# A two-layer block with gated attention and mixtures of experts: how the rows of the sparse layer travel to their experts and back

## The chip, the cores and the metric

One core of one Trainium2 chip. The metric is the device time of one execution in microseconds, the median of the runs shown. Engines by the names of the profile: PE (TensorE, matmuls), PEld (its weight load), DVE (VectorE), ACT (ScalarE), POOL (GpSimd), SP (SyncE, which issues most DMAs). A row "SPq" or "PEldq" is the sequencer of that engine.

## The reference

`x` is 4 x 256 rows of 256 numbers (T = 1024 rows). Four steps follow, each of the form x = x + tanh(g) * f(layernorm(x)): an adjacency attention and a mixture of 8 experts with a shared one (layer 0), then a latent attention of 16 heads and a mixture of 16 experts with a shared one (layer 1). The last step is the one that the change concerns:

```python
scores = jax.nn.sigmoid(x @ gate_w)
_, selected = jax.lax.top_k(scores + expert_bias[None, :], 2)
top_scores = jnp.take_along_axis(scores, selected, axis=1)
top_scores = top_scores / (top_scores.sum(-1, keepdims=True) + 1e-20)
shared = jax.nn.silu(x @ shared_gate_w) * (x @ shared_up_w) @ shared_down_w
comb = jnp.zeros((T, E), jnp.float32).at[jnp.arange(T)[:, None], selected].add(top_scores)
for e in range(E):                     # E = 16, F = 128
    g, u = jnp.split(x @ experts_gate_up[e], 2, axis=-1)
    routed = routed + comb[:, e:e + 1] * (jax.nn.silu(g) * u @ experts_down[e])
return shared + routed
```

## The kernel before

Everything is written out by hand: one program per engine, with semaphores between them, so the order of each engine is the order of the code. `x` lives in SBUF as 8 tiles of 128 rows (`NT` = 8); a half is 4 tiles. Layer 0 and the attention of layer 1 run first. The attention is a loop over 8 pairs of heads in 12 slots each (`run_pairs`); functions in a dictionary are hung into single slots of the first or last pass. Slot 11 of the last pass holds the last output projection (`project`, L1374), its result is added to x by DVE (L1770).

The sparse layer of the second half of the program has these parts.

- **Norm and routing, by halves.** `Norm.stats`, `act_root`, `scale` (rows `xn`), `pe_transpose` (L323), `act_high` and `low` (`xT_h`, `xT_l`, two parts of fp32r that together keep the precision). `Router.pe_logits` (L374), a copy by ACT (L380), `pe_turn_logits` (L387), a sigmoid by ACT, and `choose1` on DVE, which leaves two one-hot rows for each token (`ohs`) and their sum `chosen`. In the last pass, `attention_to_ffn` hangs in slot 11: it issues the first half's logits and the gate and up matmuls of the shared expert (`ffn1.gateup`, L696) in front of the last projection.
- **Ranks and places.** `rank_pe` counts with triangular matmuls, once for both halves, how many earlier rows chose the same expert. `place` on DVE turns this into a slot in a list in which each expert owns whole blocks of 128 slots (`NBLK` = 31 blocks in all, the most that can be needed), and writes `in_blk` and `spread`, from which `rows_pe1` (L491) sums a table `rows_u`: for each block the 128 rows of x. `owners` gives for each block its expert's offset in the weights (`owner_i`).
- **Shared expert.** `gateup`, `act_silu`, `hidden`, `low`, `pe_down` (L721), `add` (L673) for each half. PE starts the blocks when the second `add` is done (`ffn1.acc`).
- **Blocks.** SP has stored the normed rows twice in DRAM (`xn_rows`). For each block POOL gathers 128 rows by index from it (L826, four buffers `moe_x`), PE transposes them (`turn`, L859), multiplies by gate and up (`gateup`, L870), transposes the hidden rows (`turn_hidden`, L879) and projects down (`down`, L886); ACT and DVE stand between. The weights of all experts are in SBUF, and PE finds a block's by a register. Four registers at a time are loaded from SBUF (L897) in front of `gateup` of blocks 0, 4, 8, ...; each value is checked at run time against its limits. PE issues block b's `gateup`, `turn_hidden(b-1)`, `down(b-2)`, `turn(b+2)`. ACT writes the result (`moe_y`, four buffers, L927) and SP stores it to DRAM (`y_rows`, L842).
- **End.** When all stores have landed, POOL gathers 16 times 128 rows by slot, two for each token tile (L835). DVE multiplies them by the routing weights and adds them to x (`combine`, L964, L969), and SP stores the output in four pieces (L979).

## Time and profile before

| | us |
|---|---|
| median of 3 runs | 642.78 |
| the runs | 644.35, 642.78, 639.86 |
| the profiled execution, its own time | 644.12 |
| its span, first to last instruction | 642.3 |

| engine | busy us | share of the span |
|---|---|---|
| PE | 539.5 | 84% |
| PEld | 392.2 | 61% |
| DVE | 433.3 | 67% |
| ACT | 293.1 | 46% |
| POOL | 158.2 | 25% |

The busy times are those of the whole span, in which stages with different limits follow one another. The page gives further the chain of work that ended last, with the share of each engine in it, and the DMAs with their time from issue to landing. The trace behind it can be asked for stretches and single lines.

### The profile page before, as it was taken

What the parts mean: (1) busy time and instruction counts of PE and PEld (TensorE: products, weight loads), DVE (VectorE), ACT (ScalarE), POOL (GpSimd) and SP (SyncE); (2) the same over time, 40 slices, a digit from 0 to 9 for tenths busy, and PEclk for the clock granted to TensorE, in tenths of its full rate; (3) what the DMA queues carried; (4) which work ended last, traced back from release to release, by engine and by line L of the source; (5) the groups of instructions that cost most, each with busy time, mean ns of one, the idle gap of its engine ahead of it and who ended that gap; (6) DMA issues with size and microseconds to landing.
All of it is one profiled execution on the core that took longest, in us unless ns stands there. A gap on an engine that the chain in (4) does not pass through costs nothing.

```text
span 642.3 us, 9412 instructions
## 1 busy us (share of the span) xinstructions
PE 539.5 (84%) x2822; PEld 392.2 (61%) x2822; DVE 433.3 (67%) x1152; ACT 293.1 (46%) x753; POOL 158.2 (25%) x161
## 2 busy tenths in 40 slices
PE   6797999987889989999999999999988672799900
PEld 3574687764678865666666666666656442677700
DVE  5997289985465656979787979797878557322213
ACT  3844433335365523545554655464547340255400
POOL 1043156642245512101010101010000011455254
PEclk9868899997889999999999999999998856699965
DMA  7669022221313220101010101000045110134233
GB/s 261 206 225 337 21 73 74 75 66 36 113 35 98 82 82 25 34 26 35 24 33 24 33 24 33 24 0 1 1 180 229 65 66 3 47 112 127 75 106 115
DMA packets 25440, 51.80 MB, mean 81 GB/s; under 512 B 4211, under 2 KB 15421, under 8 KB 25024
## 3 DMA queue, kind: packets, MB, share of 16 engines
q1 hardware_dynamic: 23152, 47.20, 22.2%
q0 software_dynamic: 2256, 4.20, 2.5%
q8 instruction: 16, 0.26, 0.2%
q14 instruction: 16, 0.13, 0.1%
HBM read 40.63 MB, written 12.71 MB: 83 GB/s over the span
## 4 chain that ended last, share of the span: by engine, by line
PE 63%; DVE 19%; ACT 7%; issue 6%; DMA 2%; POOL 2%; POOLq 0%; DVEq 0%; SPq 0%; ACTq 0%
PE bank L1306 10%; PE bank L1324 9%; PE bank L696 8%; PE bank L870 5%; PE bank L1347 5%; PE bank L1357 3%; PE bank L721 3%; DVE left L1704 3%; PE bank L1374 2%; PE bank L886 2%; DVE best L1699 2%; PE bank L1205 2%; PE bank L1338 2%; PE bank L1214 2%; PE bank L374 1%
## 5 line engine op out<-in xcount | busy, mean ns | idle before, releaser
L1522 ACT ACTIVATE silu<-bank,negm 128x256 f32<-128x256 f32 x128 | 59.4, 473 | 37.5 <-DVE negm L1751 37.3
L1530 ACT ACTIVATE probsT<-bank 128x512 f32<-128x512 f32 x64 | 38.4, 600 | 60.9 <-PE bank L1347 60.9
L1324 PE MATMUL bank<-qr,att_w_raw 128*64 128x512 f32 (+1 forms) x192 | 61.9, 605 | 1.2 <-issue 1.2
L1168 POOL TENSOR_TENSOR att_w_l<-att_w_raw,att_w_h 128x384 fp32r<-128x384 f32 x16 | 16.2, 1020 | 167.0 <-ACT att_w_h L1546 167.0
L618 POOL TENSOR_TENSOR ffn_w_l<-ffn_raw,ffn_w_h 128x512 fp32r<-128x512 f32 x30 | 38.7, 1290 | 72.0 <-ACT ffn_w_h L630 57.1
L642 ACT ACTIVATE hid_h<-hid 128x512 fp32r<-128x512 f32 x30 | 18.9, 631 | 67.8 <-DVE hid L657 48.4
L1759 DVE TENSOR_SCALAR hid<-silu,rden 128x256 f32<-128x256 f32 x128 | 47.6, 414 | 2.3
L1347 PEld LDWEIGHTS bank<-ident,hid 128*128 128x128 f32 x256 | 29.2, 142 | 28.3 <-issue 19.2
L1347 PE MATMUL bank<-ident,hid 128*128 128x128 f32 x256 | 40.8, 283 | 5.6 <-DVE hid L1759 2.8
L1751 DVE TENSOR_REDUCE negm<-bank 128x2 f32<-128x512 f32 x64 | 43.6, 682 | 2.2 <-PE bank L1339 1.3
L624 POOL TENSOR_TENSOR ffn_w_l<-ffn_raw,ffn_w_h 128x256 fp32r<-128x256 f32 x30 | 22.9, 765 | 88.4 <-ACT ffn_w_h L634 88.4
L696 PE MATMUL bank<-xT_h,ffn_w_h 128*128 128x512 f32 x120 | 44.2, 454 | 0.0
L826 POOL DMA_INDIRECT moe_x<-xn_rows,route_rows x31 | 31.1, 1004 | 43.3 <-DVE route_rows L545 16.9
L696 PE MATMUL bank<-xT_l,ffn_w_h 128*128 128x512 f32 x120 | 41.8, 432 | 0.0
L1770 DVE SCALAR_TENSOR_TENSOR x<-bank,tg,x 128x512 f32<-128x512 f32 x32 | 23.8, 744 | 21.5 <-PE bank L1374 21.5
L1338 PE MATMUL bank<-ks_h,qs 128*128 128x256 f32 x128 | 36.9, 310 | 1.6 <-ACT silu L1522 1.6
L721 PE MATMUL bank<-ffn_w_h,hid_h 128*128 128x256 f32 x120 | 31.5, 294 | 7.9 <-DVE x L673 4.4
L870 PE MATMUL bank<-moe_w,moe_xT 128*128 x124 | 34.5, 403 | 3.9 <-issue 2.4
L1737 DVE TENSOR_TENSOR qr<-bank,cosq 128x512 f32<-128x512 f32 x48 | 33.0, 687 | 5.0 <-PE bank L1306 4.6
L655 DVE TENSOR_TENSOR silu<-silu,bank 128x512 f32<-128x512 f32 x22 | 15.1, 686 | 31.3 <-ACT rows L447 16.5
L951 DVE COPY moe_hidT<-bank 128x128 f32<-128x128 f32 x31 | 9.0, 292 | 39.3 <-PE bank L879 39.3
L1357 PE MATMUL bank<-probsT,kv 128*64 128x256 f32 x256 | 35.4, 398 | 0.0
(217 smaller groups left out, 1357.9 us busy)
## 6 DMA issues: line engine op xcount, KB each, us to landing
ffn_raw<-in_w_ffn SPq DMA_DIRECT2D x30, 256.0 KB, 2.6
pair_w<-in_pair_w SPq DMA_DIRECT2D x8, 768.0 KB, 5.6
moe_w<-in_w_moe SPq DMA_DIRECT2D x2, 3072.0 KB, 14.0
folds<-att_w_raw SPq DMA_DIRECT2D x6, 896.0 KB, 6.8
att_w_raw<-folds SPq DMA_DIRECT2D x12, 384.0 KB, 3.1
y_rows<-moe_y SPq DMA_DIRECT2D x31, 128.0 KB, 1.8
ffn_raw<-in_w_ffn SPq DMA_DIRECT2D x30, 128.0 KB, 2.3
xn_rows<-xn SPq DMA_DIRECT2D x4, 512.0 KB, 3.5
```

Of the source, the lines that this page charges most:

```text
L618: nc.gpsimd.tensor_tensor(wt_l[b][:, 0:GU], raw[b][:, 0:GU], wt_h[b][:, 0:GU], ALU.subtract).then_inc(self.wgl, 1)
L696: last = nc.tensor.matmul(bank[2 * st.b + g][:], wp[st.b][:, (2 * kt + g) * P:(2 * kt + g + 1) * P], xp[:, kt, st.hf * 512:(st.hf + 1) * 512],
L721: last = nc.tensor.matmul(bank[4 + t // 2][:, (t % 2) * D:(t % 2 + 1) * D], hp[st.b][:, t * P:(t + 1) * P], wp[st.b][:, GU:WC], start=(sel ...
L870: last = nc.tensor.matmul(bank[2 + b % 2][:, 0:2 * P], xgT[b % 2][:, k, :], cells[:, bass.ds(cell + k * 2 * P, 2 * P)], start=(k == 0), st ...
L1306: last = nc.tensor.matmul(bank[bk][:], m_of(wp[b], k, j), xp[:, k, c * 512:(c + 1) * 512], start=(m == 0), stop=(m == 5))
L1324: last = nc.tensor.matmul(bank[2][cols, :], g_of(w_raw[b], 2 * j + w)[:, cols], qr[n % JT][:, w, :], start=(first and w == 0), stop=(not f ...
L1338: nc.tensor.matmul(o, q, ks_h[:, keys], start=True, stop=False)
L1347: last = nc.tensor.matmul(bank[6][:, (2 * h + k) * P:(2 * h + k + 1) * P], pn[u % 2][:, h, k * P:(k + 1) * P], ident[:], start=True, stop= ...
L1357: last = nc.tensor.matmul(bank[7][h * C:(h + 1) * C, 0:S], kv[:, 2 * b + k, 0:C], pT2[b % 2][:, h, k, :], start=(k == 0), stop=(k == 1), s ...
L1522: last = nc.scalar.activation(ex[u % 2][:, h, :], bank[4 + u % 2][:, h * S:(h + 1) * S], ACT.Exp, bias=negm[:, u % 2, h:h + 1], accum_out= ...
L1751: nc.vector.tensor_reduce(negm[:, u % 2, :], bank[4 + u % 2][:].rearrange("p (h n) -> p h n", h=2), AX_X, ALU.max, negate=True).then_inc(s ...
L1759: last = nc.vector.tensor_scalar(pn[u % 2][:, h, :], ex[u % 2][:, h, :], rden[:, u % 2, h:h + 1], None, ALU.mult)
```

## The change

The attention is untouched. In the sparse layer:

- The normed rows are no longer stored twice in order and gathered by block. DRAM now holds `xn_slots`, 16 regions of 1024 rows, one for each expert. Each row is scattered by POOL to its expert's region at its rank (16 indexed DMAs from SBUF, two for each tile). The place needs only ranks, so it is worked out by halves (`slots`), and `rank_pe` runs by halves too.
- A block is then 128 consecutive rows of a region. SP loads it with a plain DMA whose address is in a register (`row_at`, from a longer `owners`), four registers at a time.
- As a region is not full, it is cleared before: 8 DMAs of 2 MB from one blank tile, issued by SP, two in front of the loop over pairs and six in it.
- A block's result is scattered by POOL with the table `rows_u` straight to the token's row of `y_rows`; lanes without a row have an index over the limit and are left out. The 16 gathers at the end become 8 plain DMAs of 256 KB from SP.
- `rows_u` is still summed by PE, now in bf16 from two values in one matmul (`blk_val`), and is needed by the first scatter of results only. `spread` is one operation instead of 16.
- The register loads have no run-time check, and PE's next four stand behind `down(b-2)`.
- The last projection of the attention comes in front of the first half's logits and shared-expert matmuls, the orders of PE, ACT and DVE around it are as in the diff, and the expert weights come in one DMA instead of two. PE waits for `ffn1.acc` as before.

```diff
-        xn2 = nc.dram_tensor("xn_rows", (2 * T, D), F32, kind="Internal").ap()
-        y2 = nc.dram_tensor("y_rows", (NBLK * P, D), F32, kind="Internal").ap()
+        xn2 = nc.dram_tensor("xn_slots", (E1 * T, D), F32, kind="Internal").ap()
+        y2 = nc.dram_tensor("y_rows", (2 * T, D), F32, kind="Internal").ap()
...
-        def rank_pe(pe):
...
+        def rank_pe(pe, hf):
+
+            pe.wait_ge(s_chosen, hf + 1)
+            ps, t0 = ranks[hf], 4 * hf
+            nc.tensor.matmul(ps[:, 0:4, :], tri[:, 0:P], chosen[:, t0:t0 + 4, :], start=True, stop=False,
+                             skip_group_check=True)
...
+        def slots(dve, seq, hf):
+
+            ts = slice(4 * hf, 4 * hf + 4)
+            dve.wait_ge(s_rank, hf + 1)
             dve.wait_ge(s_cst, 16)
-            ranks = bank[0][:, 0:NT * E1].rearrange("p (t e) -> p t e", e=E1)
-            count = bank[0][:, NT * E1:(NT + 1) * E1]
+            seq.link(nc.vector.tensor_tensor(
+                capv[:, ts, :], ranks[hf][:, 0:4, :],
+                cst[:, C_CAP:C_CAP + E1].unsqueeze(1).broadcast_to([P, 4, E1]), ALU.add))
+            seq.link(nc.vector.tensor_tensor(
+                smul[:, ts, :, :], ohs[:, ts, :, :], capv[:, ts, :].unsqueeze(2).broadcast_to([P, 4, 2, E1]),
+                ALU.mult))
+            cs = slice(8 * hf, 8 * hf + 8)
+            seq.link(nc.vector.tensor_reduce(slot_of[:, cs], smul[:, ts, :, :].rearrange("p t j e -> p (t j) e"),
+                                             AX_X, ALU.add))
+            nc.vector.tensor_copy(slot_u[:, cs], slot_of[:, cs]).then_inc(s_slot, 1)
...
-            for c in range(2 * NT):
-                last = nc.vector.tensor_scalar(spread[:, c, :], cst[:, C_LANE:C_LANE + P], lane[:, c:c + 1],
-                                               cst[:, C_ROW + c:C_ROW + c + 1], ALU.is_equal, ALU.mult)
-            last.then_inc(s_spread, 1)
...
+            nc.vector.tensor_tensor(
+                spread[:], cst[:, C_LANE:C_LANE + P].unsqueeze(1).broadcast_to([P, 2 * NT, P]),
+                lane[:].unsqueeze(2).broadcast_to([P, 2 * NT, P]), ALU.is_equal).then_inc(s_spread, 1)
...
-            def clear(self, pool):
-                for i in range(NGB):
-                    nc.gpsimd.memset(xg[i][:], 0.0).then_inc(s_xg0, 1)
-
-            def gather(self, pool, b):
-                if b >= NGB:
-                    pool.wait_ge(s_mt, b - NGB + 1)
+            def place(self, pool, hf):
+
+                pool.wait_ge(s_clr, 16 * CLEARS)
...
+                for t in range(4 * hf, 4 * hf + 4):
+                    for c in (2 * t, 2 * t + 1):
+                        nc.gpsimd.indirect_dma_start(
+                            xn2, bass.IndirectOffsetOnAxis(ap=slot_u[:, c:c + 1], axis=0), xn[:, t, :], None,
+                            bounds_check=E1 * T - 1, oob_is_err=False).then_inc(s_xsc, 16)
+
+            def scatter(self, pool, b):
...
                 nc.gpsimd.indirect_dma_start(
-                    xg[b % NGB][:], None, xn2, bass.IndirectOffsetOnAxis(ap=rows_u[:, b:b + 1], axis=0),
-                    bounds_check=2 * T - 1, oob_is_err=False).then_inc(s_xg[b % NGB], 16)
-
-            def fetch(self, pool):
-                for i in range(NYB):
-                    pool.wait_ge(s_ysc[i], 16 * len(range(i, NBLK, NYB)))
-                for t in range(NT):
-                    for j in range(2):
-                        nc.gpsimd.indirect_dma_start(
-                            yback[j][:, t, :], None, y2,
-                            bass.IndirectOffsetOnAxis(ap=slot_u[:, 2 * t + j:2 * t + j + 1], axis=0),
-                            bounds_check=NBLK * P - 1, oob_is_err=False).then_inc(s_back[t // 2], 16)
-
-            def store(self, sp, b):
-                sp.wait_ge(s_my, b + 1)
-                sp.dma_start(y2[b * P:(b + 1) * P, :], ysb[b % NYB][:]).then_inc(s_ysc[b % NYB], 16)
+                    y2, bass.IndirectOffsetOnAxis(ap=rows_u[:, b:b + 1], axis=0), ysb[b % NYB][:], None,
+                    bounds_check=2 * T - 1, oob_is_err=False).then_inc(s_ysc[b % NYB], 16)
 
             def prog_pool(self, pool):
+                self.place(pool, 0)
+                self.place(pool, 1)
                 pool.wait_ge(s_row_of, 1)
...
-                self.fetch(pool)
+                for b in range(NBLK):
+                    self.scatter(pool, b)
+
+            def values(self, eng, at, b, top):
+                n = min(4, NBLK - b)
+                _, got = nc.values_load_multi_w_load_instructions(
+                    at[0:1, b:b + n], engines=[eng], min_val=0, max_val=top,
+                    skip_runtime_bounds_check_because="the value is held under its limit by the minimum before it")
+                return {b + i: v for i, v in enumerate(got)}
+
+            def prog_sp(self, sp):
+                sp.wait_ge(s_owner, 1)
+                row = {}
+                for b in range(NBLK):
+                    if b % 4 == 0:
+                        row.update(self.values(mybir.EngineType.SP, row_at, b, E1 * T - P))
+                    if b == 0:
+                        sp.wait_ge(s_xsc, 16 * 2 * NT)
+                    if b >= NGB:
+                        sp.wait_ge(s_mt, b - NGB + 1)
+                    sp.dma_start(xg[b % NGB][:], xn2[bass.ds(row[b], P), :]).then_inc(s_xg[b % NGB], 16)
...
+                pe.wait_ge(s_cell, 16)
                 pe.wait_ge(s_owner, 1)
-                cell = {}
+                cell = self.values(mybir.EngineType.PE, cell_at, 0, (E1 - 1) * CELL)
                 self.turn(pe, 0)
...
-                    if b % 4 == 0 and b < NBLK:
-                        n = min(4, NBLK - b)
-                        _, got = nc.values_load_multi_w_load_instructions(
-                            owner_i[0:1, b:b + n], engines=[mybir.EngineType.PE], min_val=0,
-                            max_val=(E1 - 1) * CELL)
-                        cell.update({b + i: v for i, v in enumerate(got)})
...
+                    if b % 4 == 3 and b + 1 < NBLK:
+                        cell.update(self.values(mybir.EngineType.PE, cell_at, b + 1, (E1 - 1) * CELL))
...
-                for b in range(NBLK):
-                    self.store(sp, b)
+                for i in range(NYB):
+                    sp.wait_ge(s_ysc[i], 16 * len(range(i, NBLK, NYB)))
+                for g in range(NT // 2):
+                    for j in range(2):
+                        sp.dma_start(yback[j][:, 2 * g:2 * g + 2, :],
+                                     y2[j * T + 2 * g * P:j * T + 2 * (g + 1) * P, :].rearrange(
+                                         "(t p) d -> p t d", p=P)).then_inc(s_back[g], 16)
...
+                def clear_slots(i):
+                    sp.dma_start(xn2.rearrange("(c p n) d -> c p n d", c=CLEARS, p=P)[i],
+                                 blank[:].unsqueeze(1).broadcast_to([P, E1 * T // P // CLEARS, D])).then_inc(s_clr, 16)
+                sp.wait_ge(s_zz, 2)
+                for i in range(NPAIR - 2, CLEARS):
+                    clear_slots(i)
                 with sp.Fori(0, (NPAIR - 2) // 2) as ii:
...
+                        clear_slots(ii * 2 + b)
...
-                def store_rows(hf):
...
-                    sp.dma_start(cells[:, cols], a["w_moe1"][:, cols]).then_inc(s_cell[c], 16)
-                for c in range(E1 // CHUNK):
-                    load_cells(c)
-                store_rows(0)
-                store_rows(1)
+                sp.dma_start(cells[:], a["w_moe1"]).then_inc(s_cell, 16)
+                blocks.prog_sp(sp)
...
-                def attention_to_ffn():
-                    route[1][0].pe_logits(pe)
-                    route[1][0].pe_turn_logits(pe)
-                    ffn1.gateup(pe, ffn1_first)
                 run_pairs(slot, pe, {Q3_AT - 1: lambda: n_att[1].pe_transpose(pe),
                                      Q3_AT: lambda: n_att[1].pe_whole(pe)},
-                          {10: lambda: n_ffn1[0].pe_transpose(pe), 11: attention_to_ffn})
-                pe.wait_ge(route[1][0].act, 1)
-                pe.wait_ge(s_xa, NPAIR * B + 1)
+                          {10: lambda: n_ffn1[0].pe_transpose(pe)})
+                route[1][0].pe_logits(pe)
+                route[1][0].pe_turn_logits(pe)
+                ffn1.gateup(pe, ffn1_first)
                 n_ffn1[1].pe_transpose(pe)
+                rank_pe(pe, 0)
                 route[1][1].pe_logits(pe)
                 route[1][1].pe_turn_logits(pe)
+                pe.wait_ge(s_slot, 1)
+                rank_pe(pe, 1)
                 ffn1.gateup(pe, ffn1_second)
-                pe.wait_ge(ffn1.hid, 1)
-                rank_pe(pe)
                 ffn1.pe_down(pe, ffn1_first)
                 rows_pe1(pe)
                 ffn1.pe_down(pe, ffn1_second)
-                pe.wait_ge(s_row_of, 1)
...
-
-                def route_first_half():
-                    route[1][0].act_logits(act)
-                    route1_act(route[1][0], act)
+                    ffn1.split_down(act, ffn1_second)
...
                 n_ffn1[1].act_root(act)
+                route[1][0].act_logits(act)
+                route1_act(route[1][0], act)
                 n_ffn1[1].act_high(act)
                 route[1][1].act_logits(act)
                 route1_act(route[1][1], act)
-                ffn1.split_down(act, ffn1_second)
...
                 dve.wait_ge(s_xa, NPAIR * B + 1)
+                dve.wait_ge(s_rp, NPAIR * 2 * JT)
                 n_ffn1[1].stats(seq)
+                n_ffn1[1].scale(dve, seq)
                 choose1(route[1][0], dve, seq)
-                n_ffn1[1].scale(dve, seq)
                 n_ffn1[1].low(dve)
+                slots(dve, seq, 0)
                 choose1(route[1][1], dve, seq)
+                slots(dve, seq, 1)
+                compact(dve, seq)
                 ffn1.hidden(dve, ffn1_first)
+                owners(seq)
                 ffn1.low(dve, nc.vector, ffn1_first)
                 place(dve, seq)
                 ffn1.hidden(dve, ffn1_second)
+                ffn1.add(dve, ffn1_first)
                 rows_of(dve, seq)
-                owners(seq)
                 ffn1.low(dve, nc.vector, ffn1_second)
-                ffn1.add(dve, ffn1_first)
```

Left out are names, buffers and constants, `compact` (the first four operations of the old `place`), the rest of `owners` (seven more operations on one partition: the first row of each block's region) and of `place` (`off` and `slotv` from `capv`, then as before, and `blk_val`, one product over 992 elements).

Where the order changes, first on PE at the end of the attention. L1357 and L1404 are the same line of the last values product, L1374 and L1421 the last projection, L374 and L384 the logits, L387 and L397 their transposes, L696 and L743 the shared expert's gate and up. Before:

```order
L1357 MATMUL bank<-probsT,kv 64x256 x4
L374 MATMUL bank<-xT_h,rg_h 16x512 x2
L374 MATMUL bank<-xT_h,rg_l 16x512 x2
L374 MATMUL bank<-xT_l,rg_h 16x512 x2
L387 MATMUL bank<-ident,lgT 128x16 x4
L696 MATMUL bank<-xT_h,ffn_w_h 128x512 x2
L696 MATMUL bank<-xT_l,ffn_w_h 128x512 x2
L696 MATMUL bank<-xT_h,ffn_w_h 128x512 x2
L696 MATMUL bank<-xT_l,ffn_w_h 128x512 x2
L696 MATMUL bank<-xT_h,ffn_w_l 128x512 x4
L1374 MATMUL bank<-att_f_h,c_h 128x256
L1374 MATMUL bank<-att_f_l,c_h 128x256
```

After:

```order
L1404 MATMUL bank<-probsT,kv 64x256 x4
L1421 MATMUL bank<-att_f_h,c_h 128x256
L1421 MATMUL bank<-att_f_l,c_h 128x256
L1421 MATMUL bank<-att_f_h,c_h 128x256
L1421 MATMUL bank<-att_f_l,c_h 128x256
L1421 MATMUL bank<-att_f_h,c_l 128x256 x2
L384 MATMUL bank<-xT_h,rg_h 16x512 x2
L384 MATMUL bank<-xT_h,rg_l 16x512 x2
L384 MATMUL bank<-xT_l,rg_h 16x512 x2
L397 MATMUL bank<-ident,lgT 128x16 x4
L743 MATMUL bank<-xT_h,ffn_w_h 128x512 x2
```

The projection's six matmuls moved up, in front of the first half's logits.

Second, on PE in the blocks around the second load of registers (`bank<-ident,moe_hid` is `turn_hidden`, `bank<-moe_w,moe_hidT` is `down`, `bank<-ident,moe_x` is `turn`; ISA rows work out an address). Before:

```order
L879 MATMUL bank<-ident,moe_hid 128x128
L886 ISA
L886 MATMUL bank<-moe_w,moe_hidT 128x256
L859 MATMUL bank<-ident,moe_x 128x128 x2
L897 TENSOR_LOAD route_owner_at
L897 ISA x8
L870 ISA
L870 MATMUL bank<-moe_w,moe_xT 128x256
```

After:

```order
L931 MATMUL bank<-ident,moe_hid 128x128
L938 ISA
L938 MATMUL bank<-moe_w,moe_hidT 128x256
L891 TENSOR_LOAD route_cell_at
L913 MATMUL bank<-ident,moe_x 128x128 x2
L922 ISA
L922 MATMUL bank<-moe_w,moe_xT 128x256
```

The load moved from behind `turn` to between `down` and `turn`, and the eight instructions behind it are gone.

Third, on SP after the loop over pairs. Before:

```order
L1123 DMA route_const<-in_route 128x472
L1136 DMA moe_w<-in_w_moe 128x6144 x2
L1130 DMA xn_rows<-xn 128x4x256 x4
L842 DMA y_rows<-moe_y 128x256 x31
L979 DMA out<-x 128x512 x4
```

After, the first block loads:

```order
L1185 DMA route_const<-in_route 128x503
L1187 DMA moe_w<-in_w_moe 128x12288
L891 TENSOR_LOAD route_row_at
L906 ISA
L906 DMA moe_x<-xn_slots 128x256
L906 ISA
L906 DMA moe_x<-xn_slots 128x256
```

SP's stores of rows and of results are gone from its order, and each load of a block, with an address worked out, has come in; 31 in all, and behind them the 8 loads of `y_rows`.

## Rows read from the trace of the kernel before

**Rows 1.** The page: who carries the chain that ended last.

```profile
PE 63%; DVE 19%; ACT 7%; issue 6%; DMA 2%; POOL 2%; POOLq 0%; DVEq 0%; SPq 0%; ACTq 0%
```

**Rows 2.** Stretches: PE, PEld, DVE, ACT, POOL busy (instructions), granted clock, DMA share, GB/s.

```profile
510.20:551.20 41.00, 18.31 (x79) 14.05 (x79) 26.68 (x103) 7.42 (x12) 5.94 (x9) 0.62 0.11 34
551.20:611.50 60.30, 55.69 (x279) 44.44 (x279) 16.83 (x69) 29.40 (x93) 26.92 (x27) 0.95 0.31 94
611.50:642.30 30.80, 0.00 (x0) 0.00 (x0) 6.71 (x16) 0.04 (x1) 16.25 (x16) 0.56 0.38 111
```

**Rows 3.** Timeline, end of attention: start, us, engine, line, operation [idle before <-releaser].

```profile
503.08 0.64 PE L374 MATMUL bank<-xT_h,rg_h 128*16 128x512 f32 x2
...
503.62 0.42 DVE L1765 TENSOR_TENSOR c_l<-bank,c_h 128x256 fp32r<-128x256 f32 x1 [0.83 <-ACT c_h L1536]
...
505.67 0.73 PE L696 MATMUL bank<-xT_h,ffn_w_h 128*128 128x512 f32 x2
...
509.05 0.39 PE L1374 MATMUL bank<-att_f_h,c_l 128*128 128x256 f32 x2
509.48 0.75 DVE L1770 SCALAR_TENSOR_TENSOR x<-bank,tg,x 128x512 f32<-128x512 f32 x1 [5.43 <-PE bank L1374]
```

**Rows 4.** Timeline, routing of the second half of the tokens.

```profile
512.32 0.20 ACT L296 ACTIVATE root<-var 128x4 f32<-128x4 f32 x1 [4.21 <-DVE var L291]
...
516.23 1.94 PE L323 MATMUL bank<-ident,xn 128*128 128x128 f32 x8 [6.79 <-DVE xn L308]
...
522.97 1.28 ACT L451 ACT_TABLE_LOAD   x1
...
527.05 0.23 DVE L472 TENSOR_TENSOR chosen<-one_hots 128x64 bf16<-128x64 f32 x1
```

**Rows 5.** Timeline, DVE in the placement and the shared expert.

```profile
534.28 4.19 DVE L525 TENSOR_SCALAR route_spread<-route_const,route_lane 128x128 fp32r<-128x128 f32 x16
...
542.75 0.67 DVE L533 TENSOR_TENSOR route_below<-route_ends,route_const 1x496 f32<-1x496 f32 x1
...
549.49 1.66 DVE L673 SCALAR_TENSOR_TENSOR x<-bank,tg,x 128x256 f32<-128x256 f32 x4 [3.02 <-PE bank L721]
```

**Rows 6.** Timeline, PE, gate and up matmuls of three blocks in a row.

```profile
572.05 1.03 PE L870 MATMUL bank<-moe_w,moe_xT 128*128 x4
...
573.67 1.03 PE L870 MATMUL bank<-moe_w,moe_xT 128*128 x4
...
575.88 0.48 PE L870 MATMUL bank<-moe_w,moe_xT 128*128 x1 [0.42 <-issue]
```

**Rows 7.** Line L897, PE's own sequencer: duration ns min/median/max.

```profile
L897 PEldq FUSED_REGOPS  x31: 146/146/165, 552.0 to 604.2; - x31
...
L897 PEldq TENSOR_LOAD <-route_owner_at x8: 328/336/776, 551.4 to 602.8; - x8
```

**Rows 8.** Timeline, last y of ACT, last gather of POOL, the DVE it released.

```profile
611.16 0.38 ACT L927 ACTIVATE moe_y<-bank 128x256 f32<-128x256 f32 x1 [0.21 <-PE bank L886]
...
633.76 1.22 POOL L835 DMA_INDIRECT moe_back<-y_rows,route_slot_at  x1 [0.30 <-issue]
637.76 0.88 DVE L964 SCALAR_TENSOR_TENSOR x<-xn,pick_weight,x 128x256 f32<-128x256 f32 x2 [3.65 <-DMA moe_back<-y_rows,route_slot_at]
```

**Rows 9.** DMA issues: destination<-source, count, KB each, median us to landing.

```profile
folds<-att_w_raw SPq DMA_DIRECT2D x6, 896.0 KB, 6.8
...
y_rows<-moe_y SPq DMA_DIRECT2D x31, 128.0 KB, 1.8
...
xn_rows<-xn SPq DMA_DIRECT2D x4, 512.0 KB, 3.5
...
out<-x SPq DMA_DIRECT2D x4, 256.0 KB, 2.6
```

**Rows 10.** Timeline, SP's load of folded weights and ACT's next use of that buffer.

```profile
235.44 0.34 SPq L1094 DMA_DIRECT2D att_w_raw<-folds  x1
...
263.81 0.53 ACT L1546 ACTIVATE att_w_h<-att_w_raw 128x384 fp32r<-128x384 f32 x1
```

164 lines of the change are left out of this document (89 added, 75 removed).

## The prediction

> **What bounds the kernel now.** I read the page first [rows 1]: of the chain that ended last TensorE (PE) carries 63%, VectorE (DVE) 19%. That is an average over stages. The change touches the last 140 us, so I cut those by the table of stretches [rows 2] and see three different kernels. From 510.2 to 551.2 (routing and the shared expert) PE is busy 18.3 us of 41, at a granted clock of 0.62, and DVE 26.7: a relay in which each engine waits for the other. From 551.2 to 611.5 (31 expert blocks) PE is busy 55.7 of 60.3: PE-bound. From 611.5 to the end nothing computes but 6.7 us of DVE: the 16 gathers on POOL and their landings set the time. The run itself took 644.12 us, 1.8 outside the span, and stands 1.3 above the median 642.78.
>
> **1. The last projection is no longer behind the first half's routing.** Before, PE does the logits from 503.08 and 12 shared-expert matmuls from 505.67, and only then L1374, though its input c_l was done at 504.04; the add into x starts at 509.48 [rows 3]. After, L1374 stands first (first pair of order rows in front). Its two matmuls on c_l take 0.39, so the add starts near 504.04 + 0.39 + 0.07 of handing over = 504.5. **-5.0 us**, x ready at 505.25.
>
> **2. From x to the second half's expert choice.** Before: 510.23 to 527.28, 17.05 us [rows 3, 4]. After: statistics and root 2.35 (510.23 to 512.52 before [rows 3, 4]); then ScalarE (ACT) hands over the first logits 0.6, PE turns them 0.45, and the 12 matmuls (3.0: from 505.67 until four of L1374, 0.12 apart, could start in front of 509.05 [rows 3]) now stand in front of the transposes of the second half. Transposes: 1.94 before, where they also waited; four fifths of that, 1.5. Rounding to xT_h and xT_l 1.3; logits 2.3, a guess between the first half's pace (two of the six take 0.64) and nearly twice that at the lower clock of this stretch [rows 2, 3]; copy, turn and sigmoid 1.4; choosing 2.75 (table load to 524.25, sigmoid 0.25, choice done at 527.28 [rows 4]). Sum 15.65. The sigmoid table load, 1.28 us [rows 4], is gone there, since the first sigmoid comes later and no square root stands between the two. **-1.4**, with 1.5 either way for the clock. The first half's choice and slots() run on DVE in the shadow of PE.
>
> **3. From the choice to the release of the blocks.** Before: 527.28 to 551.15, 23.9 us. After, in DVE's order: rank and slots() 2.0; compact() 1.5; hidden 0.7; owners(), now in front of place(): four operations over 496 elements at 0.67 (two before) and seven small ones at 0.2, 4.1 [rows 5]; low 0.7; place() 7.1: 3.55 until in_blk (three operations of 0.7, two of 0.45, two small), then blk_val over 992 elements, 1.15 (a fixed part beside twice the 496 of L533), lane 0.2, and one spread over 2048 elements, 2.2 at the same 1 ns an element, for 16 pieces that took 4.19 [rows 5]. Hidden 0.7, add 1.65. In their shadow PE sums the rows with 16 matmuls, now of bf16. rows_of() 0.8, low 0.7. PE's second down projection needs that last low; 4 matmuls of 12 remain behind it, 1.3. The last add 1.66. Sum 22.9, **-1.0**, so PE is free for the blocks at 543.8 instead of 551.15.
>
> Can the blocks' inputs be there? slots(0) ends near 515.3. POOL then issues 16 scatters. No row shows a scatter; the nearest is the gather, 1.0 busy (16.25 us for 16 [rows 2]) and 0.30 between two [rows 8]. 16 x 1.3 = 20.8, the last starts at 534.8 and lands 4.0 later (as the last gather, 633.76 to 637.76 [rows 8]); SyncE (SP) reads its registers meanwhile, loads the first block (128 KB; a store of that size lands in 1.8 [rows 9]) by 541.2. Under 543.8, by 2.6 us. This cover is thin: above 1.46 us per scatter it is gone and each 0.1 us costs 1.6.
>
> **4. In the blocks.** A period without a load of registers is 1.62 us (572.05 to 573.67), one with it 2.21 (573.67 to 575.88) [rows 6]: 0.59 lost at every fourth block, seven times. PE's sequencer shows why: a TENSOR_LOAD of 336 ns and, for each of the 31 values, a bounds instruction of 146 ns [rows 7], 0.92 us per four blocks, of which the queued matmuls cover 0.33. The change drops the bounds instructions and moves the load in front of the transposes, behind the down projection (second pair of order rows). What is left, 0.34, is as much as the cover: I take all, 7 x 0.6 = **-4.2** (bounds 0 and 4.2). At the head the first load, up to 0.78, is in front of the first transposes instead of in the wait for xT: **-0.2**.
>
> The page "DMA: Bandwidth & Descriptors" of the Trainium skill (Latency and other measured facts) gives a register load a floor of about 600 ns. The trace does not agree, its median is 336 ns [rows 7]; by the page the stall would shrink only to 0.27 and the sum would come out 1.9 us higher.
>
> POOL now writes 31 results with indices where SP stored them, and SP loads where POOL gathered. Queued behind each scatter is only the next one. 1.3 is less than 1.63, so POOL keeps up; ACT rewrites one of four y buffers after 6.5 us, and the scatter has landed 4.0 after POOL begins it, if it is like the last gather [rows 8]. Cover 2.5 us. SP's load of block b+4 starts when block b is turned, and has 6.5 us for about 2.
>
> **5. The end.** Before: last y at 611.54, end 642.3: 30.8 us: 16 gathers at 1.3 in a row, each group of four followed by 1.7 of DVE, then one 256 KB store, 2.9 to the end [rows 8]. After: the last four y come 1.6, 1.4, 1.0 and 0.6 us apart, faster than POOL's 1.3: 1.0 late. Scatter to landing 4.0 (best 2.8: POOL's 1.0 and the 1.8 of a plain store). Eight plain loads of 256 KB from SP: by landing times 2.6 for 256 KB and 3.5 for 512 [rows 9], 1.7 + 8 x 0.9 = 8.9. Last add 1.7, store and end 2.95. Sum 18.6, **-12.2** (bounds -8, see D, and -14.4, with no lateness and the best landing).
>
> **6. What it adds elsewhere.** Eight clears of 2 MB each from one blank tile. Two are issued at 236.3, in front of the folded weights that SP loads at 235.44 now and ACT needs at 263.81 [rows 10]. 4.2 MB at 176 GB/s (896 KB in 6.8 - 1.7 us, the slowest store here [rows 9]) is 23.9 us, and 2.8 for the folds: 263.0. Just hidden; at the slope of the 256 and 512 KB rows, 290 GB/s, by 10 us. The other six follow a load that is needed 20 us later or more. **0**, bound +24, see C. Two more ACT copies ahead of waits (0.35 and 0.41 us) and odds: **+0.8**.
>
> Sum: -5.0 - 1.4 - 1.0 - 0.2 - 4.2 - 12.2 + 0.8 = -23.2. Against the profiled run 644.1 - 23.2 = 620.9, against the median 619.6. I say 620.
>
> **Rivals.**
> *A, slower than before: an indexed write is dear on POOL.* 16 stand in front of the blocks and 31 in them. With x us each the time is 515.3 + 16x + 6.3 (landing, first load) + 31x + 9 (head and drain) + 18.6 + 1.8 = 551 + 47x once x is over 1.63. It reaches 644 at x = 2.0; at 2.6 it is 673. For it: descriptors go to scattered rows of DRAM. Against it: the gather's 1.0 us is the same work with the two sides exchanged [rows 2]. The same page (Anatomy of one DMA) holds that the receipt of the last write makes most of a DMA's fixed 2 us and that DRAM is the slowest target; the 128 KB stores to DRAM here land in 1.8 us [rows 9], so that alone would not do it. Chance 0.03.
> *B, the scatters end later than the shared expert.* At 1.7 us each they and the load end at 548.8, 5.0 later, and the blocks run at 1.7: near 628. Chance 0.11.
> *C, the clears delay the attention.* At half the slowest store rate seen the folds come 24 us late once: 630 to 643. For it: all 16 pieces that a partition writes in a clear read the same 1 KB, which no row shows. Chance 0.06.
> *D, the end gives back less:* landing of scattered rows 6 us and 2 MB in 14 us: some 7 less, 627. Chance 0.08.
> *E, nothing gained in the relay:* the steps 2 to 4 bring 0 since the wait for the register and the lower clock stay as they are: 627. Chance 0.06.
>
> **How the numbers follow.** The forecast has 0.66, its own range 615 to 626. B, D and E end at 627 to 628, A and C outside. Range 613 to 629, with some 0.13 left out. A measurement of this kernel tells 1% (6.4 us) from nothing. Over 1% faster is all but A, the upper part of C and a rest: 0.93. Within 1%: 0.04. Slower: 0.03.
>
> **What would show it.** The add into x some 5 us earlier; no sigmoid table load in the second half; the first block's transposes near 544 to 545, released by the add and not by a moe_x load; blocks 1.63 apart with no step at every fourth; POOL's scatters near 1.0 + 0.3; the end 18 to 19 us after the last y; folds' first use at the same time after the attention starts. It would be wrong first through the scatter's price, then through the clears.

## The result, and the profile after

The change makes the kernel faster. The median of four runs is 613.39 us (612.98 to 618.09), beside 641.32 for the kernel before on the same chip (639.40 to 644.35): a ratio of 0.958, with an interval from 0.953 to 0.964. A fifth run on record, outside that median, took 615.63. The forecast was 620 in a range from 613 to 629: the median lies 0.4 us inside the lower end of the range, and below the forecast's own inner range of 615 to 626. The profiled execution took 618.09 us with a span of 616.2, where the profiled one of before had 642.3: 26.1 less, and the sum of the prediction had said 23.2 less.

The page of the kernel after, the chain by engine (beside [rows 1]), and the table of stretches, cut at the same events as [rows 2] (end of the add into x, release of the blocks, last y, end). The columns are those of [rows 2].

```profile
PE 62%; DVE 18%; ACT 7%; issue 6%; DMA 3%; POOL 3%; SPq 0%; DVEq 0%; POOLq 0%; ACTq 0%
```

```profile
505.50:543.30 37.80, 20.05 (x102) 15.20 (x100) 29.36 (x105) 7.82 (x13) 17.61 (x16) 0.74 0.18 61
543.30:597.90 54.60, 53.16 (x279) 43.57 (x279) 16.91 (x70) 29.55 (x93) 28.08 (x29) 0.96 0.37 111
597.90:616.20 18.30, 0.00 (x0) 0.00 (x0) 6.51 (x16) 0.00 (x0) 2.04 (x3) 0.61 0.52 172
```

The three stretches were 41.0, 60.3 and 30.8 us and are 37.8, 54.6 and 18.3. The first is still a relay (PE busy 20.1 of 37.8), the second is PE's even more than before (53.2 of 54.6, where it was 55.7 of 60.3), and in the third VectorE does what it did before, 6.5 us, in little more than half the time. POOL is busy 17.6 us in the first stretch, where it had 5.9: the sixteen scatters.

c_l is VectorE's last operation in front of the last projection (L1806). It starts at 503.67, and at 503.62 before [rows 3], so that the times in these two traces can be compared directly. That is partly chance, as the repeated runs below show. From c_l on I cut both by the same events. Each column of the table is the time from the mark before it; a mark is the start of an operation, but for the second add and the last y, which count by their ends. "The choice" is the start of the operation that writes `chosen` for the second half.

| kernel (one trace each) | c_l to add into x | to second half's choice | to the second add's end | to the first gate matmul | to last y | to the end | c_l to end |
|---|---|---|---|---|---|---|---|
| before | 5.86 | 17.57 | 24.10 | 2.21 | 58.18 | 30.76 | 138.68 |
| after | 1.10 | 15.97 | 22.58 | 1.89 | 52.67 | 18.32 | 112.53 |
| difference | -4.8 | -1.6 | -1.5 | -0.3 | -5.5 | -12.4 | -26.15 |
| predicted (steps 1 to 5) | -5.0 | -1.4 | -1.0 | -0.2 | -4.2 | -12.2 | -24.0 |

The timelines of the kernel after from which the first columns come (start, us, engine, line, operation, idle time before it and what ended it). VectorE and PE between the end of the attention and the choice:

```profile
503.67 0.42 DVE L1806 TENSOR_TENSOR c_l<-bank,c_h 128x256 fp32r<-128x256 f32 x1 [0.89 <-ACT c_h L1580]
...
504.77 0.75 DVE L1811 SCALAR_TENSOR_TENSOR x<-bank,tg,x 128x512 f32<-128x512 f32 x1 [0.68 <-PE bank L1421]
...
508.70 0.73 PE L743 MATMUL bank<-xT_h,ffn_w_h 128*128 128x512 f32 x2
508.86 1.38 DVE L318 TENSOR_SCALAR xn<-x,mv,rstd 128x256 f32<-128x256 f32 x4
...
513.10 1.08 PE L333 MATMUL bank<-ident,xn 128*128 128x128 f32 x8
...
515.76 0.64 PE L384 MATMUL bank<-xT_h,rg_h 128*16 128x512 f32 x2 [1.49 <-DVE xT_l L349]
...
518.45 0.22 ACT L461 ACTIVATE sc<-bank 128x64 f32<-128x64 f32 x1 [0.51 <-PE bank L397]
...
520.74 0.23 DVE L482 TENSOR_TENSOR chosen<-one_hots 128x64 bf16<-128x64 f32 x1
```

L1421 is the last projection; it stands right behind c_l, and the add into x that it releases starts at 504.77, 4.7 earlier than in [rows 3]. The sigmoid at 518.45 (L461) waits for PE alone and has no table load in front of it, unlike [rows 4].

POOL's scatters and VectorE beside them, and the end of the relay:

```profile
532.02 0.97 POOL L872 DMA_INDIRECT xn_slots<-xn,route_slot_at  x1 [0.30 <-issue]
...
532.86 1.19 DVE L576 TENSOR_TENSOR route_blk_val<-route_in_blk,route_const 128x992 bf16<-128x992 f32 x1
533.30 1.60 POOL L872 DMA_INDIRECT xn_slots<-xn,route_slot_at  x1 [0.30 <-issue]
...
534.17 2.29 DVE L582 TENSOR_TENSOR route_spread<-route_const,route_lane 128x2048 bf16<-128x2048 f32 x1
535.21 2.11 POOL L872 DMA_INDIRECT xn_slots<-xn,route_slot_at  x1 [0.30 <-issue]
...
541.66 1.66 DVE L720 SCALAR_TENSOR_TENSOR x<-bank,tg,x 128x256 f32<-128x256 f32 x4 [1.79 <-PE bank L768]
...
544.00 1.09 PE L913 MATMUL bank<-ident,moe_x 128*128 128x128 f32 x4 [2.37 <-DMA moe_x<-xn_slots]
```

The first row of the transposes names the load of moe_x as what ended their wait. The prediction had said that this would be the sign of a relay without cover. The experiments show that the row misleads here (part 3).

The end of the program: the last y, the last scatter, SP's loads and VectorE's adds.

```profile
597.50 0.38 ACT L976 ACTIVATE moe_y<-bank 128x256 f32<-128x256 f32 x1 [0.21 <-PE bank L938]
...
599.57 0.97 POOL L878 DMA_INDIRECT y_rows<-moe_y,route_rows  x1 [0.30 <-issue]
601.79 0.39 SPq L1028 DMA_DIRECT2D xn<-y_rows  x1
...
605.37 0.88 DVE L1013 SCALAR_TENSOR_TENSOR x<-xn,pick_weight,x 128x256 f32<-128x256 f32 x2 [8.74 <-DMA moe_back<-y_rows]
...
608.51 0.88 DVE L1013 SCALAR_TENSOR_TENSOR x<-xn,pick_weight,x 128x256 f32<-128x256 f32 x2 [1.47 <-DMA moe_back<-y_rows]
```

### The profile page after: what moved, and what is told of

Its sections match the earlier page's. It is cut to its first block, busy times and chain, and to the rows that moved or that the text cites. A ratio compares the mean times of both kernels' runs of the same rounds, so it can differ in the third digit from the quotient of the medians.

```text
span 616.2 us, 9452 instructions
## 1 busy us (share of the span) xinstructions
PE 534.0 (87%) x2826; PEld 388.4 (63%) x2826; DVE 435.7 (71%) x1154; ACT 290.5 (47%) x751; POOL 158.4 (26%) x158
## 4 chain that ended last, share of the span: by engine, by line
PE 62%; DVE 18%; ACT 7%; issue 6%; DMA 3%; POOL 3%; SPq 0%; DVEq 0%; POOLq 0%; ACTq 0%
PE bank L1353 10%; PE bank L1371 10%; PE bank L743 8%; PE bank L1394 5%; PE bank L922 5%; PE bank L1404 4%; DVE left L1745 3%; PE bank L768 3%; PE bank L1421 3%; PE bank L938 2%; DVE best L1740 2%; POOL xn_slots L872 2%; PE bank L1252 2%; PE bank L1261 2%; PE bank L1385 2%
## 5 line engine op out<-in xcount | busy, mean ns | idle before, releaser
L1371 PE MATMUL bank<-qr,att_w_raw 128*64 128x512 f32 (+1 forms) x192 | 63.5, 614 | 1.2 <-issue 1.2
L743 PE MATMUL bank<-xT_h,ffn_w_h 128*128 128x512 f32 x120 | 42.9, 441 | 0.0
L743 PE MATMUL bank<-xT_l,ffn_w_h 128*128 128x512 f32 x120 | 41.3, 428 | 0.0
L878 POOL DMA_INDIRECT y_rows<-moe_y,route_rows x31 | 30.1, 972 | 30.6 <-issue 19.0
L743 PE MATMUL bank<-xT_h,ffn_w_l 128*128 128x512 f32 x120 | 35.8, 423 | 1.1 <-POOL ffn_w_l L665 1.1
L1404 PE MATMUL bank<-probsT,kv 128*64 128x256 f32 x256 | 35.5, 399 | 0.0
L1371 PEld LDWEIGHTS bank<-qr,att_w_raw 128*64 128x64 f32 (+1 forms) x192 | 19.3, 156 | 24.8 <-issue 21.5
L1353 PE MATMUL bank<-xT_h,att_w_h 128*128 128x512 f32 x96 | 33.6, 431 | 0.4 <-DVE qr L1778 0.3
## 6 DMA issues: line engine op xcount, KB each, us to landing
moe_w<-in_w_moe SPq DMA_DIRECT2D x1, 6144.0 KB, 18.3
```

The lines of the kernel that those rows point to most:

```text
L743: last = nc.tensor.matmul(bank[2 * st.b + g][:], wp[st.b][:, (2 * kt + g) * P:(2 * kt + g + 1) * P], xp[:, kt, st.hf * 512:(st.hf + 1) * 512],
L1353: last = nc.tensor.matmul(bank[bk][:], m_of(wp[b], k, j), xp[:, k, c * 512:(c + 1) * 512], start=(m == 0), stop=(m == 5))
L1371: last = nc.tensor.matmul(bank[2][cols, :], g_of(w_raw[b], 2 * j + w)[:, cols], qr[n % JT][:, w, :], start=(first and w == 0), stop=(not f ...
L1404: last = nc.tensor.matmul(bank[7][h * C:(h + 1) * C, 0:S], kv[:, 2 * b + k, 0:C], pT2[b % 2][:, h, k, :], start=(k == 0), stop=(k == 1), s ...
```

## The experiments

Twelve kernels follow, on three chips: a0 to a3, b0 to b3 and c1 to c4. Those of one letter share a chip and the runs of the kernel before. Two of the twelve are the changed kernel again, as the thing to compare with; c1 to c4 have none on their chip and are compared with a0 and b0. Single runs of one kernel differ by up to 8 us (c3, 636.40 to 644.17), while in the three traces of the changed kernel each stretch behind c_l agrees within 0.35. So the verdicts rest on the traces, of which each kernel has one, and the times stand beside them.

| kernel | median, us | ratio to before (95%) | c_l to add | to choice | to second add | to gate matmul | to last y | to end | c_l to end |
|---|---|---|---|---|---|---|---|---|---|
| after, again (a0) | 617.48 | 0.958 (0.955 to 0.961) | 1.10 | 15.95 | 22.59 | 1.89 | 52.37 | 18.64 | 112.54 |
| after, again (b0) | 614.41 | 0.956 (0.952 to 0.960) | 1.11 | 15.95 | 22.57 | 1.88 | 52.34 | 18.56 | 112.41 |
| projection behind (a1) | 620.40 | 0.965 (0.962 to 0.968) | 5.86 | 15.81 | 22.53 | 1.89 | 53.46 | 18.15 | 117.70 |
| two scatters more (a2) | 619.39 | 0.962 (0.957 to 0.966) | 1.10 | 15.95 | 22.58 | 4.04 | 53.01 | 18.22 | 114.90 |
| eight scatters more (a3) | 625.65 | 0.971 (0.967 to 0.975) | 1.10 | 15.94 | 22.57 | 11.71 | 52.60 | 18.35 | 122.27 |
| gathers at the end (b1) | 629.15 | 0.978 (0.975 to 0.982) | 1.09 | 15.96 | 22.56 | 1.89 | 52.69 | 31.76 | 125.95 |
| logits first (b2) | 613.30 | 0.952 (0.948 to 0.956) | 1.10 | 15.03 | 22.99 | 1.88 | 52.65 | 17.62 | 111.27 |
| and end on two queues (b3) | 612.90 | 0.954 (0.949 to 0.958) | 1.10 | 15.03 | 22.96 | 1.88 | 52.69 | 17.19 | 110.85 |
| old stall (c1) | 622.49 | 0.971 (0.967 to 0.975) | 1.11 | 15.97 | 22.58 | 3.06 | 58.52 | 18.68 | 119.92 |
| checks back, place kept (c2) | 620.27 | 0.969 (0.964 to 0.974) | 1.10 | 15.95 | 22.58 | 3.11 | 58.42 | 18.15 | 119.31 |
| clears in front (c3) | 639.48 | 0.996 (0.993 to 0.999) | 1.09 | 15.95 | 22.58 | 1.89 | 52.34 | 18.35 | 112.20 |
| shared expert first (c4) | 615.74 | 0.961 (0.958 to 0.963) | 1.10 | 15.03 | 25.96 | 1.30 | 53.43 | 17.38 | 114.20 |

### The changed kernel again

> The changed kernel once more, on the chip of the three kernels that run beside it. By its own median against the kernel before (613.4 against 641.3): 27.9 us faster, 613 to 614.

> The changed kernel on the chip of the three kernels beside it: 613 to 618, and 113.9 us from the last attention context's matmuls (502.6 in its trace) to the end, as in the two traces of it so far.

Both agree with the first trace behind c_l within 0.15 us. In front of it they don't: c_l comes at 503.96 in a0 and at 497.89 in b0, and the ratio of the medians to the kernel before is nearly the same for both (0.958 and 0.956). The tables of stretches of a0 and of b0 show where the 6 us lie:

```profile
0.00:100.00 100.00, 84.38 (x384) 62.38 (x385) 71.27 (x256) 47.77 (x114) 29.40 (x31) 0.86 0.56 180
100.00:200.00 100.00, 86.06 (x421) 66.73 (x420) 73.27 (x200) 45.12 (x83) 43.18 (x41) 0.91 0.25 72
```

```profile
0.00:100.00 100.00, 84.35 (x408) 62.58 (x409) 77.21 (x271) 49.81 (x118) 32.77 (x34) 0.93 0.55 184
100.00:200.00 100.00, 85.22 (x436) 65.62 (x435) 72.49 (x191) 46.39 (x85) 43.56 (x42) 0.97 0.25 75
```

The granted clock is 0.86 and 0.91 in the first two stretches of a0, and 0.93 and 0.97 in b0, for the same program. So a single profiled span tells nothing of a difference of 1%, while the stretch behind a common event does. The traces also bear on the stretch in front of c_l: in each of the five stretches from 0 to 490 a0 has the granted clock of the trace of before (0.86, 0.91, 1.00, 1.00, 0.98), and its c_l comes 0.34 us later than there.

### Part 1 and 2: the projection and the logits

The last attention projection behind the first half's routing again (PE; ScalarE's sigmoid follows in the same way):

```diff
-                          {10: lambda: n_ffn1[0].pe_transpose(pe)})
-                route[1][0].pe_logits(pe)
-                route[1][0].pe_turn_logits(pe)
-                ffn1.gateup(pe, ffn1_first)
+                          {10: lambda: n_ffn1[0].pe_transpose(pe), 11: attention_to_ffn})
```

> The changed kernel with the rearrangement around the last projection undone: the first half's logits and the shared expert's first tile stand ahead of the last attention projection again, and ScalarE's sigmoid of the first half with them. Everything behind the add into x is that of the change. Theory (the choice of the second half is on the path that ends last, all the way to the blocks): what the two traces gave, the add into x 4.7 us later (509.48 against 504.77) and the stretch from it to the choice 16.8 to 17.0 us in place of 15.45, so 4.7 + 1.4 = 6.1 us slower than the changed kernel, 619 to 620. Rival (POOL's relay of sixteen scatters and the landing of the last one end after the shared expert's work, so an earlier choice is partly lost behind them): the relay starts with the first half's slots, not with the choice, so these move by less; then 2 to 4 us slower, 615.5 to 617.5.

Measured from c_l: 5.2 us slower (117.70 against 112.5). By the medians it is 2.9 (620.40 against 617.48), and without the profiled runs (that of a1 had its c_l at 498.00, early as in b0) 4.5 by the means, 621.3 against 616.8. The times alone would not exclude the rival's 2 to 4; the trace does: the add into x moved by 4.76, and 4.6 of it are still there at the second add, so next to nothing is lost behind POOL's relay. The first theory (6.1) is nearer, but had its parts wrong. The stretch from x to the choice, which should have grown by 1.4, became 0.14 shorter. Another 0.9 us is in the blocks, where the second block is still at the lower of the two levels of PE's clock (1.91 us in place of 1.03). The rows of a1:

```profile
503.86 0.75 DVE L1814 SCALAR_TENSOR_TENSOR x<-bank,tg,x 128x512 f32<-128x512 f32 x1 [5.43 <-PE bank L1421]
...
507.94 1.38 DVE L318 TENSOR_SCALAR xn<-x,mv,rstd 128x256 f32<-128x256 f32 x4
...
508.73 1.97 PE L333 MATMUL bank<-ident,xn 128*128 128x128 f32 x8 [4.91 <-DVE xn L318]
...
512.72 1.03 PE L384 MATMUL bank<-xT_h,rg_h 128*16 128x512 f32 x2 [0.88 <-DVE xT_l L349]
...
516.11 1.28 ACT L461 ACT_TABLE_LOAD   x1
```

VectorE scales xn 4.08 us after the start of the add into x, as in the kernel after (508.86 against 504.77). In the kernel before it was 5.87 after it:

```profile
515.35 1.38 DVE L308 TENSOR_SCALAR xn<-x,mv,rstd 128x256 f32<-128x256 f32 x4
```

There the first half's choice stood in between (512.20 to 514.43). The difference, 1.79 us, is the whole of step 2 (17.57 in the kernel before, 15.81 in a1, which differ in this stretch mainly by the order on VectorE). So the gain of step 2 is that new order, the norm in front of the first half's choice; no run puts that order back by itself. What the prediction had put there, the table load of 1.28 us that is saved and the twelve matmuls that are added, weigh each other out: in a1 the matmuls are out of the way and the transposes start at once, but they take 1.97 in place of 1.08, two logits take 1.03 in place of 0.64, and the table load stands on the path.

The next kernel takes the twelve matmuls out of the way:

```diff
                 route[1][0].pe_turn_logits(pe)
-                ffn1.gateup(pe, ffn1_first)
                 n_ffn1[1].pe_transpose(pe)
                 rank_pe(pe, 0)
                 route[1][1].pe_logits(pe)
                 route[1][1].pe_turn_logits(pe)
+                ffn1.gateup(pe, ffn1_first)
```

> The changed kernel, but on PE the second half's transposes, the rank of the first half and the second half's logits stand in front of the shared expert's first tile of gate and up matmuls (in the trace after, xn is there near 509.7 and the transposes start at 513.10, behind those twelve matmuls). VectorE's order is the same: the first half's choice (done at 512.40) stands in front of the rounding xT_l, so the logits start near 513.8 in place of 515.76. Theory (the path goes through the second half's choice and through the first half's slots, both 1.9 us earlier): 1.9 us faster than the changed kernel. Rival (the twelve matmuls now end behind the logits, and the granted clock falls before the transposes and logits since PE idles before them: six logits at 1.05 for two in place of 0.63, transposes at 1.9 in place of 1.1): the gain is eaten, 0 to 0.5 us, or the shared expert becomes late, +1.

From c_l it is 1.1 to 1.3 us faster. But up to the first gate matmul it is only 0.5 (39.9 against 40.4), the size of the rival, and for the reason that the rival gives:

```profile
507.22 1.89 PE L333 MATMUL bank<-ident,xn 128*128 128x128 f32 x8 [0.89 <-DVE xn L318]
...
511.22 1.03 PE L384 MATMUL bank<-xT_h,rg_h 128*16 128x512 f32 x2 [0.88 <-DVE xT_l L349]
```

The transposes start 4.9 us after the add into x, in place of 8.3, yet take 1.89, and two logits take 1.03 to 1.05: PE is on the lower of its two levels here (granted clock 0.54 from 507.2 to 509.2 and 0.50 from 511.2 to 514.0). The choice comes 0.94 us earlier and not 1.9, 0.4 of it is lost again in the relay, and 0.7 to 1.0 appears at the end, where this kernel's second group of adds waits 0.6 us and not 1.5 to 1.8. Nothing in the edit explains this last part, so it isn't shown to be the edit's. The times (0.952 and 0.956, with overlapping intervals) can't tell the two kernels apart.

### Part 3: does POOL's relay have cover?

```diff
+                if hf == 1:
+                    for c in range(2):
+                        nc.gpsimd.indirect_dma_start(
+                            xn3, bass.IndirectOffsetOnAxis(ap=slot_u[:, c:c + 1], axis=0), xn[:, c // 2, :], None,
+                            bounds_check=E1 * T - 1, oob_is_err=False).then_inc(s_xsc, 16)
...
-                        sp.wait_ge(s_xsc, 16 * 2 * NT)
+                        sp.wait_ge(s_xsc, 16 * (2 * NT + 2))
```

> The changed kernel with two more indexed scatters (rows of x, again by the same slots, into a DRAM buffer of their own) behind the sixteen and ahead of the load of the first block: 2 x 1.27 = 2.54 us more in POOL's relay. Theory of the trace after (the first block's transposes at 544.00 were released by the load of moe_x, not by the add at 543.32, so the cover of the relay is spent): +1.9 to +2.5 us on the changed kernel, 615.5 to 616. The prediction's own reading (2.6 us of cover): 0 us, 613.4.

> As the kernel with two more scatters, with eight: 8 x 1.27 = 10.2 us more in POOL's relay. Theory (no cover left): +9.5 to +10.2 us, 623 to 624. With the predicted 2.6 us of cover: +7.6, 621. If the scatters overlap with their landing or cost more than POOL's own time (queue full), the step per scatter, taken between this kernel and the one with two, differs from 1.27 us.

The two scatters put the first gate matmul 2.15 us later and the eight 9.82. The step between the two kernels is (11.71 - 4.04) / 6 = 1.28 us per scatter, POOL's own time and pause. The cover is what two scatters didn't show of their 2.54: 0.4 us; by the eight, 10.2 - 9.82, the same. So neither 2.6 nor nothing. The last scatter and the first transposes of the kernel with eight more:

```profile
547.04 0.97 POOL L878 DMA_INDIRECT xn_more<-xn,route_slot_at  x1 [0.30 <-issue]
549.61 1.90 SPq L912 DMA_DIRECT2D moe_x<-xn_slots  x4
...
551.71 0.69 PE L919 MATMUL bank<-ident,moe_x 128*128 128x128 f32 x2 [12.17 <-DMA moe_x<-xn_slots]
```

From the start of the last scatter to the transposes it is 4.67 us (4.66 in a2): 2.6 until SP may issue the load, 2.1 for it. In the kernel after this distance is 5.10 (538.90 to 544.00) and in the kernel with the logits first 6.37, with the transposes 0.67 after the second add in both. That is PE's register load: it starts at 543.4, right behind the add at 543.32, takes 0.52, and the transposes follow. So they were not waiting for moe_x, whatever the row says: the load had landed 0.4 us before. POOL's relay was simply within half a microsecond of being the bound. (That the load had landed is worked out from the 4.67 of the other two traces.)

### Part 4: the stalls in the blocks

The bounds instructions back on PE's register loads (c2), and besides the load put back in front of gate and up (c1):

```diff
+                why = None if eng == mybir.EngineType.PE else "the value is held ..."
...
-                    skip_runtime_bounds_check_because="the value is held ...")
+                    skip_runtime_bounds_check_because=why)
```

```diff
+                    if b % 4 == 0 and 0 < b < NBLK:
+                        cell.update(self.values(mybir.EngineType.PE, cell_at, b, (E1 - 1) * CELL))
                     if b < NBLK:
                         self.gateup(pe, b, cell[b])
...
-                    if b % 4 == 3 and b + 1 < NBLK:
-                        cell.update(self.values(mybir.EngineType.PE, cell_at, b + 1, (E1 - 1) * CELL))
```

> The changed kernel with PE's register loads as before the change: the load of four values in front of the gate and up matmuls of the first block that needs them, with a bounds instruction for each value. From the first gate matmul to the last y the changed kernel takes 52.4 to 52.7 us in three traces, the kernel before 58.2. Theory (the seven stalls of 0.6 are the gain, and the rest of the 5.5 us is the clock that rose one block earlier, 1.2): +4.2 us, 56.6 to 56.9. Rival (the stalls were the whole 5.5, or something else in the blocks, as SP's plain stores): +5.5, or clearly under +4.

> The changed kernel with the bounds instructions on PE's register loads, but the loads left behind the down projection and in front of the transposes. Prediction's reading (the place only covers as much as the old one, 0.33 us of 0.92): nearly all of the 4.2 us comes back, +3.5 to +4.2. Rival (the place is what counts: the transposes of block b+2 are needed a whole block later, so a stall in front of them is absorbed): 0 to +1.0, and the periods show no step at every fourth block.

Both come out the same and dearer than any theory had it: 6.1 and 6.0 us in the blocks and 1.2 more ahead of them, 7.2 to 7.3 us in all. With 58.52 and 58.42 us the blocks are as long as in the kernel before (58.18), so the checks and the clock are all of the gain there, and SP's loads and POOL's scatters in place of POOL's gathers and SP's stores neither gave nor cost anything that shows. Where these instructions run, the place of the load is worth nothing (0.1); the load put late without them wasn't tried. Line L892 of the kernel with the checks back, in the 2 us in front of the blocks (PEldq is PE's sequencer; durations in ns, then the first and the last start), and its gate and up matmuls:

```profile
L892 PEldq FUSED_REGOPS  x4: 146/151/165, 539.6 to 540.5; - x4
L892 PEldq SEQ_ASSERT  x4: 18/18/28, 539.8 to 540.7; - x4
...
L892 PEldq TENSOR_LOAD <-route_cell_at x1: 517/517/517, 539.0 to 539.0; - x1
```

```profile
544.32 1.91 PE L923 MATMUL bank<-moe_w,moe_xT 128*128 x4
...
555.20 1.03 PE L923 MATMUL bank<-moe_w,moe_xT 128*128 x4
...
557.46 1.10 PE L923 MATMUL bank<-moe_w,moe_xT 128*128 x4
```

Four bounds instructions start between 539.6 and 540.5: one every 0.3 us. The duration of 146 ns is only half of what one costs, because an assert of 18 ns and the steps between them belong to it. A load of four values thus holds PE's sequencer 0.34 + 4 x 0.3 = 1.5 us and not 0.92. The period that holds such a load is 2.26 us (555.20 to 557.46), where the kernel after has 1.63 from its third block on, and the head pays its 1.2 in full. The rest is the clock: the second block's matmuls take 1.91 us, as in the kernel before, and 1.03 in the kernel after. That is 1.0 us once. The granted clock is 0.50 there (544.3 to 546.2), and 1.00 in the kernel after (547.4 to 549.0). Rows of the kernel after for comparison:

```profile
547.41 1.03 PE L922 MATMUL bank<-moe_w,moe_xT 128*128 x4
...
550.24 1.03 PE L922 MATMUL bank<-moe_w,moe_xT 128*128 x4
...
551.86 1.03 PE L922 MATMUL bank<-moe_w,moe_xT 128*128 x4
```

Whether the clock rises one block earlier is not a matter of the checks alone: in a1, without checks, the second block is slow too (its blocks take 53.46). What decides it stays open.

### Part 5: the end

The old way back (POOL stores each block in order, sixteen gathers at the end):

```diff
-                nc.gpsimd.indirect_dma_start(
-                    y2, bass.IndirectOffsetOnAxis(ap=rows_u[:, b:b + 1], axis=0), ysb[b % NYB][:], None,
-                    bounds_check=2 * T - 1, oob_is_err=False).then_inc(s_ysc[b % NYB], 16)
+                pool.dma_start(y2[b * P:(b + 1) * P, :], ysb[b % NYB][:]).then_inc(s_ysc[b % NYB], 16)
...
+                for t in range(NT):
+                    for j in range(2):
+                        nc.gpsimd.indirect_dma_start(
+                            yback[j][:, t, :], None, y2,
+                            bass.IndirectOffsetOnAxis(ap=slot_b[:, 2 * t + j:2 * t + j + 1], axis=0),
+                            bounds_check=NBLK * P - 1, oob_is_err=False).then_inc(s_back[t // 2], 16)
```

> The changed kernel with the old way back: each block's result is stored by POOL in the order of the blocks, without indices, and sixteen indexed gathers (the two results of each token) are at the end, with the same adds and stores as before. Theory (the end's gain is all from this swap): the stretch from the last y to the end goes from 18.3 to 30.8, as in the kernel before: +12.2 to +12.5 us, and the blocks are the same. Rival (a part of the old end was the landing of plain stores behind SP's queue, or a part of the gain is that POOL's scatters are hidden in the blocks' time): the blocks or the end change by some other amount, +8 to +10.

The end grows from 18.6 to 31.8 us, by 13.2, and the blocks stay within 0.35 us of the kernel after. So the gain of the end is all from this swap, and the 31 scatters between the blocks cost nothing. By the times it is 14.7 us. It is 1.0 us more than in the kernel before, 0.6 of it between the last y and the first gather, where the last plain store lands, which POOL issues here and SP issued there:

```profile
596.29 1.09 POOL L892 DMA_INDIRECT xn<-y_rows,route_slot_back  x1 [2.41 <-DMA y_rows<-moe_y]
```

The last y ends at 593.04 and the first gather starts 3.25 us later (2.6 in the kernel before).

The loads at the end on two queues:

```diff
+                for i in range(NYB):
+                    act.wait_ge(s_ysc[i], 16 * len(range(i, NBLK, NYB)))
+                self.back(act, 1)
...
-                for g in range(NT // 2):
-                    for j in range(2):
-                        sp.dma_start(yback[j][:, 2 * g:2 * g + 2, :],
...
+                self.back(sp, 0)
```

> As the kernel with the logits first, and the eight loads at the end (y_rows to moe_back) issued four by SP and four by ScalarE, where SP issues all eight at 0.47 us each (601.79 to 605.8 in the trace after; the adds start at 605.37 and 608.51, then run at VectorE's own pace). If the end is bound by the issue of the loads, the second group's adds start up to 1 us earlier: 0.5 to 1.5 us faster than the kernel with the logits first. If it is bound by the landing of the first group and by VectorE behind it: 0 to 0.3 us.

```profile
597.03 1.93 SPq L1028 DMA_DIRECT2D xn<-y_rows  x4
597.03 2.01 ACTq L1028 DMA_DIRECT2D moe_back<-y_rows  x4
600.97 0.88 DVE L1016 SCALAR_TENSOR_TENSOR x<-xn,pick_weight,x 128x256 f32<-128x256 f32 x2 [9.11 <-DMA moe_back<-y_rows]
```

The eight issues are done after 2.0 us in place of 4.0, and VectorE runs through from 600.97 on. Over the one trace of the kernel with the logits first it brings 0.4 us, at the lower edge of the first theory and just over the second. That trace has the shortest end of all with one queue, though: the ten traces with the eight loads on SP alone have ends of 17.62 to 18.68, 18.3 on average, and the two with two queues (b3 and c4) 17.19 and 17.38. By these the second queue is worth some 1.0 us, inside the first theory. The times (612.90 and 613.30) can't tell. The landing of the first group (3.9 us after the issue) and VectorE's 6.4 us are most of what is left.

### Part 6: the clears

```diff
-                for i in range(NPAIR - 2, CLEARS):
+                for i in range(CLEARS):
...
-                        clear_slots(ii * 2 + b)
```

> The changed kernel with all eight clears (16.8 MB of zeros to xn_slots) in front of the attention's loop, ahead of the folded weights that ScalarE takes at 263.73. In the trace after one clear of 2 MB lands in 8.3 to 8.7 us by itself, 240 GB/s. Theory (a queue's transfers are served in order, so that the folds wait for all eight): the clears end at 233.4 + 8 x 8.5 = 301, the folds at 304, so the attention stands still for some 40 us once: +35 to +42, 650 to 658. It would show what two clears in front cost nothing for: 13 us of cover. Rival (the queues of the 16 DMA engines serve the folds beside the clears): +0 to +10.

The time is 25 us over that of the changed kernel (a ratio of 0.996 against 0.957, the average of a0 and b0, of 642.3 us): the mechanism is the first theory's, the size is not. ScalarE's wait for the folds, and the stretch of the transfer:

```profile
233.91 40.56 SPq L1169 DMA_DIRECT2D xn_slots<-blank  x8
```

```profile
287.79 0.52 ACT L1589 ACTIVATE att_w_h<-att_w_raw 128x384 fp32r<-128x384 f32 x1 [23.46 <-DMA att_w_raw<-folds]
```

```profile
235.00:285.00 50.00, 27.14 (x111) 15.18 (x109) 22.51 (x53) 10.27 (x25) 3.23 (x3) 0.79 1.03 341
```

SP could issue the load of the folds only when the eight clears were issued, at 274.9 (233.9 + 40.6, and 0.5 between), and ScalarE got them 12.9 us after that. So it is first of all SP's own queue that the clears hold, which the theory didn't say. They move at 341 GB/s, not 240. At this rate the six clears that were moved take 6 x 2.10 MB / 341 GB/s = 36.9 us, and ScalarE waited 23.5 of them. So two clears in front leave 13.4 us of cover, and rival C had the right mechanism at a price that it doesn't reach. In the kernel after, ScalarE takes the folds at 263.73, where it did at 263.81 [rows 10].

### A version that should have been better

```diff
-                place(dve, seq)
+                place_blocks(seq)
                 ffn1.hidden(dve, ffn1_second)
                 ffn1.add(dve, ffn1_first)
-                rows_of(dve, seq)
                 ffn1.low(dve, nc.vector, ffn1_second)
+                place_rows(seq)
                 ffn1.add(dve, ffn1_second)
+                rows_of(dve, seq)
```

> The kernel with the logits first and the end on two queues, and besides: on VectorE the shared expert's second half (hidden, the first add, the low part) stands in front of blk_val and spread, the second add in front of rows_of; on PE the second down projection stands in front of the rows' matmuls, and the first register load in front of the wait for the second add. Theory of the relay: it is VectorE's work that sets the second add (540.35 in the trace with the logits first, 5.70 behind the start of the last scatter), and it becomes 2.2 earlier; the blocks then start 4.66 us after the last scatter's start, as in the kernels with more scatters, so POOL's relay takes over as the bound and the gain stops at 1.7 us: 1.5 to 1.9 from the last attention context to the end (112.3 to 110.5). Rival (no bound from POOL): -2.7. Rival (the longer wait for rows or the colder PE takes it back): 0 to -0.5.

It failed. From c_l it is 3.3 us slower than the kernel with two queues and 1.7 slower than the changed kernel; every theory fell.

```profile
538.45 1.66 DVE L727 SCALAR_TENSOR_TENSOR x<-bank,tg,x 128x256 f32<-128x256 f32 x4 [5.31 <-remote]
...
545.88 0.45 PE L920 MATMUL bank<-ident,moe_x 128*128 128x128 f32 x1 [0.61 <-issue]
```

VectorE stands still for 5.3 us in front of the first add, for which PE's matmuls had been done since 530.4, and the row names no engine as releaser ("remote"). In the same kernel and in b2 and b3 ScalarE's second silu waits 3.3 us in the same way. Two things fall into VectorE's gap, a packet of 16 KB of the instruction queue (at 534) and the landing of the last scatter (before 538.0, when SP issues the load). Which of them holds the engine, if either does, isn't settled: in the kernel after such a packet is seen at 526 without a gap on VectorE. The gap alone accounts for the failure: PE's second down projection waits for that first add (540.16), and without the 5.3 us the second add would end 20.7 us behind the choice (an estimate, 25.96 - 5.31), where the plan had 20.8 (22.96 - 2.2). Whether the blocks would then have gained isn't shown.

Two of the expected steps are seen all the same: the transposes follow the second add after 0.09 us, since the register load now stands ahead of the wait (0.67 before), and POOL's sixteen scatters take 19.9 us from the first start to the last in place of 21.2. In the kernel after two of them take 1.60 and 2.11 us, beside blk_val and spread on VectorE, and with these moved behind the scatters no scatter is that slow. The rows of the kernel after show what the slow ones have in common:

```profile
525.09 0.66 DVE L545 TENSOR_TENSOR route_below<-route_ends,route_const 1x496 f32<-1x496 f32 x1
525.55 1.05 POOL L872 DMA_INDIRECT xn_slots<-xn,route_slot_at  x1 [0.30 <-issue]
...
532.16 0.67 DVE L574 TENSOR_TENSOR route_in_blk<-route_reach 128x496 f32<-128x496 f32 x1
```

Behind the first (1.17) three of the sixteen are clearly longer than 0.97: 1.05, 1.60 and 2.11. Each started while VectorE ran an operation with two inputs in SBUF (below, blk_val, spread), and each ended 0.85 or 0.86 us after that operation did (525.75 to 526.60, 534.05 to 534.90, 536.46 to 537.32). The one at 532.02 took 0.97, though in_blk ran beside it: in_blk started 0.14 after the scatter. The one at 537.62 took 0.97 too, though an add with an input from PE's bank was running and ran 1.0 us on. c4 has this as well: blk_val and spread are gone from there, and the scatter that starts 0.10 behind below takes 1.42. So it depends on which of the two starts first, and on where the operation's inputs are.

The page "SBUF — State Buffer" of the Trainium skill (SBUF: two separate sides) has a rule of this kind: VectorE and GpSimd share a pair of ports, an operation of VectorE with two inputs in SBUF competes for it with an instruction of GpSimd that reads SBUF, and whichever starts first keeps it to its end. The trace agrees where VectorE starts first. The other way round it does not: in_blk took its 0.67 us inside the scatter that had started first, as long as in the kernel before, where POOL did nothing beside it. That an indexed scatter counts as an instruction that reads SBUF is a reading of these rows.

## Why the prediction was right, point by point

The direction and the size of the two large terms (5 and 12 us) held, and so did the mechanisms of steps 1 and 5 and, but for its sizes, of step 4. The number itself is in the range with little to spare: the median of 613.39 is 0.4 us above its lower end and under the 615 to 626 that had the forecast's own chance of 0.66. The span fell by 26.1 us and not by 23.2; the 2.9 lie in the blocks (1.4), the work in front of c_l (0.75) and 0.2 to 0.5 in each of the steps 2, 3 and 5, less 0.2 in step 1.

1. **The last projection: -5.0 predicted, -4.8 measured.** The add starts 1.10 us after c_l and not 0.88. Undone, it costs the same 4.76 us, and all of it reaches the end.

2. **From x to the choice: -1.4 predicted, -1.6 measured, by other parts.** That the number is right is luck. The twelve matmuls took 4.4 us and not 3.0 (508.70 to 513.10), since the granted clock falls among them, from 1.00 (508.7 to 509.7) to 0.50 (509.8 to 513.1); the logits took 1.55 and not 2.3. The table load is gone, but a1 without this gain is as fast: the step that was missed is the new order on VectorE, which takes the first half's choice off the path (1.8 us). "In the shadow of PE" was right of it and was not counted as what it brings.

3. **From the choice to the release: -1.0 predicted, -1.5 measured.** No run undoes this part, so that its gain is read from the two traces only. The spread took 2.29 (2.2 predicted) and blk_val 1.19 (1.15). The cover of POOL's relay was the weak step, as said there: 2.6 predicted, 0.4 measured. The relay starts at 517.68 and not at 515.3 (slots(0) ends at 516.68, and POOL starts 1.0 later, which was not in the working), and it is 1.7 longer between its first and its last start (21.2 against 15 x 1.3), mostly as two scatters were slowed (by 0.6 and 1.1); against that the last scatter lets SP go after 2.6 us, not 4.0. Of rival B, the mechanism was thus 0.4 us away: two scatters more gave 2.1 us of its 8. Rival A is out: a scatter costs POOL 1.28 us, as the gather did [rows 8].

4. **The blocks: -4.2 and -0.2 predicted, -5.5 and -0.3 measured.** This is the largest error, and it has two parts: the clock rose one block earlier (1.0 us), which no term foresaw and whose cause no run shows, and the stalls were 0.67 and not 0.6 apiece ((58.18 - 1.0 - 52.5) / 7), since the period behind each is a little longer too. The reason given for them was wrong in its size: a bounds instruction costs 0.3 us, not its 146 ns, and the queued matmuls covered 0.9 of the 1.5 us, not 0.33. Thus the 0.34 that were left fitted under the cover with room to spare, and the prediction's care for the place of the load decided nothing that the runs show. The floor of about 600 ns for a register load, from the page "DMA: Bandwidth & Descriptors" of the Trainium skill (Latency and other measured facts), is not seen: the median is 336 ns in the kernel after as well.

5. **The end: -12.2 predicted, -12.4 measured, by errors that cancel.** Predicted: 1.0 late, 4.0 to the landing, 8.9 for the loads, 1.7, 2.95. Measured, from the end of the last y at 597.88: the last scatter starts 1.7 later, SP's loads are issued 2.2 after that, VectorE's adds start at 605.37 and are bound by VectorE from 608.51 on (three groups of 1.6), and from the end of the last at 613.35 it is 2.85 to the end. The step in which the loads set the pace of the whole end holds for the first two groups only.

6. **Elsewhere: +0.8 predicted, +0.05 measured.** c_l comes at the same time in these two traces, but it moves by 6 us between traces of one kernel, so that the 0.05 shows little. The fairer measure is a0, with the granted clock of before: +0.34. The clears are hidden with some 13 us to spare. The prediction's working took 896 KB in 5.1 us as 176 GB/s; counted in the same way as its 290 GB/s it is 180, which changes nothing.

The median is lower still than these terms make it: 613.4, where 642.8 - 26.1 gives 616.7. The profiled execution of the kernel after was the slowest of its four runs, 4.7 over their median, where that of before stood 1.3 over the median of its three. The spread in front of c_l that a0 and b0 show is large enough for this. The other runs have no trace, so that it isn't shown to be the cause. On the two chips of a0 and b0 the medians differ by 27.3 and 29.1 us from those of before, with intervals that reach down to 25.1 and 25.8.

## What to carry to other kernels

Undo each part by itself and compare from a common event in the trace: a step whose size is right can have the wrong cause (step 2) or errors that cancel (step 5), and a releaser that a row names can be one that came just in time (the load of moe_x). Cost a sequencer's instructions by the distance between their starts, not by their durations. When work is moved onto a queue that feeds a later stage, measure its cover by adding two more of the same: here it was 0.4 us, and an edit that takes more than that off the other branch meets it.

## What the runs showed of the hardware that was not expected

- A runtime bounds check of a register costs PE's sequencer 0.3 us, with 146 ns of it visible as one instruction and 18 as another.
- The same program takes 6 us more or less in its first 200 us, with the granted clock at 0.86 or 0.93 in the first 100.
- An indexed scatter of 128 rows of 1 KB costs POOL 0.97 + 0.30 us, and lets a waiting load on SP start 2.2 to 2.6 us after its start, earlier than the gather's 4.0 [rows 8].
- DMAs of 2 MB in pieces of 1 KB hold SP's own queue: two of them 3.98 us and the load behind them 5.0 in the kernel after, eight of them 40.6 in c3. One that follows nothing of its kind issues in 0.56 to 0.58, a plain load in 0.33 to 0.47.
- They move 341 GB/s when eight stand in a row; one by one they land in 8.3 to 8.7 us.
- An indexed scatter that starts while VectorE runs an operation with two inputs in SBUF ends 0.85 us after that operation (1.05, 1.60 and 2.11 us in place of 0.97 in the kernel after). One that starts 0.14 before such an operation keeps its 0.97.
